# Gated recurrence on one core: bases added by VectorE instead of TensorE, triangular merges moved to GpSimd

## What is computed

```python
def step(carry, inp):
    S, R = carry
    kn = k_t / jnp.maximum(jnp.linalg.norm(k_t, axis=-1, keepdims=True), 1e-12)
    pred = jnp.einsum('bhji,bhj->bhi', S, kn)
    r = jnp.clip(v_t - pred, -CLIP, CLIP)
    S = a_t[..., None] * S
    kp = jnp.einsum('bhd,bhde->bhe', kn, S)
    S = S + b_t[..., None, None] * kn[..., None] * (v_t - kp)[..., None, :]
    o = jnp.einsum('bhji,bhj->bhi', S, q_t)
    R = aR_t[..., None] * R
    kpR = jnp.einsum('bhd,bhde->bhe', kn, R)
    R = R + g_t[..., None, None] * kn[..., None] * (r - kpR)[..., None, :]
    o = o + jnp.einsum('bhji,bhj->bhi', R, q_t)
    return ((S, R), o)
```

## Time and profile before

| | before |
|---|---|
| median of 3 runs | 3105.88 us (3103.14 to 3109.36) |
| the profiled execution, its own time | 3099.7 us |
| its span, first to last instruction | 3097.9 us |
| mean granted clock of TensorE | 0.893 |
| TensorE busy, share of the span | 82% |
| VectorE, ScalarE, GpSimd busy | 68%, 46%, 19% |

### The profile page before, as it was taken

One profiled execution on the slowest core, in us unless ns is written; L12 is line 12 of the kernel. 1 busy time (PEld: TensorE's weight loads), 2 busy tenths in 40 slices (PEclk: granted clock), 3 DMA queues, 4 the chain that ended last, 5 costly groups with the idle time before them and its releaser, 6 DMA issues. The chain is left out here.

```text
span 3097.9 us, 119998 instructions
## 1 busy us (share of the span) xinstructions
PE 2553.5 (82%) x52187; PEld 1910.8 (62%) x52187; DVE 2096.4 (68%) x5265; ACT 1412.9 (46%) x3330; POOL 591.5 (19%) x656
## 2 busy tenths in 40 slices
PE   8887478999976788888888888769998997797745
PEld 6755464556556667676776766547777554575633
DVE  3447236777749888898888988446777666565742
ACT  5443133444453455444544544437777554464310
POOL 0000525556530000000000000001111441261025
PEclk9978778999988899998999999879999998898865
DMA  3200331111110000000000000002222003152013
GB/s 98 61 1 28 121 102 51 45 57 47 38 53 4 4 4 4 4 4 4 4 4 4 4 4 4 3 9 56 62 62 72 3 3 105 48 118 65 5 45 114
DMA packets 79149, 118.11 MB, mean 38 GB/s; under 512 B 11360, under 2 KB 64240, under 8 KB 78096
## 3 DMA queue, kind: packets, MB, share of 16 engines
q1 hardware_dynamic: 66992, 88.80, 9.2%
q0 software_dynamic: 11696, 22.40, 2.9%
HBM read 98.51 MB, written 16.51 MB: 37 GB/s over the span
## 5 line engine op out<-in xcount | busy, mean ns | idle before, releaser
L3114 PE MATMUL psum<-l1d_rw,l1d_cols 64*32 64x32 f32 (+2 forms) x20480 | 241.1, 214 | 91.9 <-issue 75.3
L3114 PEld LDWEIGHTS psum<-l1d_rw,l1d_cols 64*32 64x32 f32 x20480 | 209.3, 107 | 138.3 <-issue 116.0
L2469 POOL TENSOR_SCALAR l1xs_p<-l1xs_p,l1xs_col 128x257 f32<-128x257 f32 x256 | 233.8, 932 | 204.4 <-DVE l1xs_col L2425 204.4
L1740 POOL TENSOR_SCALAR X<-X,l1f_bias 128x512 f32<-128x512 f32 x4 | 6.2, 1567 | 1148.4 <-DMA l1f_bias<-in_l1f_bias 1148.4
L2390 ACT ACTIVATE l1xs_p<-psum,l1xs_col 128x257 f32<-128x257 f32 x256 | 119.4, 472 | 209.4 <-DVE l1xs_col L2420 203.1
L3372 DVE TENSOR_TENSOR l1d_rw<-l1d_rw,l1d_tots 128x1536 f32<-128x1536 f32 x96 | 143.1, 1491 | 76.0 <-PE psum L3114 75.1
L2888 ACT COPY l1d_ya<-psum 128x512 f32<-128x512 f32 x160 | 92.8, 590 | 204.7 <-PE psum L3154 203.8
L2432 DVE STREAM_TRANSPOSE l1xs_pt<-l1xs_p 128x288 f32<-128x288 f32 x256 | 122.4, 478 | 78.7 <-POOL l1xs_p L2469 78.6
L3051 PE MATMUL psum<-l1d_src,l1d_wp 128*128 128x128 f32 x1024 | 139.3, 293 | 1.3 <-ACT l1d_src L2893 1.3
L2342 PE MATMUL psum<-l1xs_keys,l1xs_qx 128*32 128x257 f32 x2048 | 134.0, 395 | 3.5 <-DVE l1xs_qx L2414 1.9
L2354 PE MATMUL psum<-l1xs_pt,l1xs_vals 32*128 32x512 f32 x1152 | 136.6, 604 | 0.0
(11 more groups left out here) (558 smaller groups left out, 6704.4 us busy)
## 6 DMA issues: line engine op xcount, KB each, us to landing
l2f_w<-in_l2f_w SPq DMA_DIRECT2D x16, 768.0 KB, 4.4
l1xs_vals<-in_ctx_strips SPq DMA_DIRECT2D x16, 576.0 KB, 3.8
l0x_ctxT<-in_ctxT SPq DMA_DIRECT2D x16, 516.0 KB, 3.8
l1xs_keys<-in_ctxT SPq DMA_DIRECT2D x16, 516.0 KB, 4.8
l2x_ctxK<-in_ctxT SPq DMA_DIRECT2D x64, 129.0 KB, 2.1
l2x_ctxV<-in_ctxT SPq DMA_DIRECT2D x64, 129.0 KB, 2.1
l1d_wp<-in_l1d_wp SPq DMA_DIRECT2D x1, 2048.0 KB, 8.2
l2f_acc<-l2f_zero SPq DMA_DIRECT2D x8, 256.0 KB, 3.6
```

Of the source, the lines that this page charges most:

```text
L2469: nc.gpsimd.tensor_scalar(p[:, t % 4, :S2], p[:, t % 4, :S2], col[:, 2, t % 4:t % 4 + 1], None, ALU.mult).then_inc(s["norm"], 1)
L3114: mm = nc.tensor.matmul(k.ps[bank0 + pr + e // per * 2][b * T:b * T + T, e % per * w:(e % per + 1) * w], cols[rr, 2 * n, e * 128 + b * T:e ...
```

## The change

The three products by the identity leave TensorE. VectorE adds the base instead: `corner` reads the PSUM bank and the base and writes `ya`, in place of ScalarE's two copies `t` and `t2`, and `clip` adds `v` before it clips, with a wait between the two. The merges leave VectorE for GpSimd, where the sums along the innermost axis become halving additions (34 instructions a tile); the sign that three of the steps carried is put into ScalarE's gather. `turn_back` on VectorE waits for GpSimd (`inverse`). `corner` stands behind `keep_s(i, 1)` and `keep_s(i, 3)`; in lap 16 `result` moves ahead of `corner`, and the clip and the second corner stand behind `turn_back`.

```diff
-             "norm", "turn", "steps", "resid", "colr", "kr")
+             "norm", "turn", "steps", "resid", "colr", "kr", "merged", "last", "inverse")
...
+            tt = nc.gpsimd.tensor_tensor
+
+            def blocks(x, m):
+
+                return (x.rearrange("p (n x) -> p n x", x=2 * m * (T + 1))[:, :, :2 * m * T]
+                        .rearrange("p n (r c) -> p n r c", c=T))
+
+            def merge(i, m):
+
+                nb, lb, xb = T // (2 * m), blocks(lt, m), blocks(xi, m)
+                lo, hi = slice(0, m), slice(m, 2 * m)
+                t5 = tmp[:, :nb * m * m * m].rearrange("p (n r c k) -> p n r c k", n=nb, r=m, c=m)
+                w4 = wmat[:, :nb * m * m].rearrange("p (n r c) -> p n r c", n=nb, r=m)
+                flat = tmp[:, :nb * m * m * m].rearrange("p (x k) -> p x k", k=m)
+                right = lambda x: x.rearrange("p n k c -> p n c k")
+                left = lambda x, r: x[:, :, r:r + 1, :].to_broadcast([128, nb, m, m])
+                step = Steps(pool, s["merged"], i, 10, {2: 0, 4: 4}[m])
+                for r in range(m):
+                    ins = tt(t5[:, :, r], left(lb[:, :, hi, lo], r), right(xb[:, :, lo, lo]), ALU.mult)
+                step(ins)
+                if m == 4:
+                    step(tt(flat[:, :, :2], flat[:, :, :2], flat[:, :, 2:], ALU.add))
+                step(tt(wmat[:, :nb * m * m], flat[:, :, 0], flat[:, :, 1], ALU.add))
+                for r in range(m):
+                    ins = tt(t5[:, :, r], left(xb[:, :, hi, hi], r), right(w4), ALU.mult)
+                step(ins)
+                if m == 4:
+                    step(tt(flat[:, :, :2], flat[:, :, :2], flat[:, :, 2:], ALU.add))
+                step(tt(xb[:, :, hi, lo], t5[:, :, :, :, 0], t5[:, :, :, :, 1], ALU.add))
+
+            def merge_last(i):
+
+                m = 8
+                lb, xb = blocks(lt, m), blocks(xi, m)
+                lo, hi = slice(0, m), slice(m, 2 * m)
+                w4 = [wmat[:, 64 * n:64 * n + 64].rearrange("p (r c) -> p r c", r=m) for n in range(2)]
+                t4 = [tmp[:, 512 * n:512 * n + 512].rearrange("p (r c k) -> p r c k", r=m, c=m) for n in range(2)]
+                flat = [tmp[:, 512 * n:512 * n + 512].rearrange("p (x k) -> p x k", k=m) for n in range(2)]
+                left = lambda x: x.unsqueeze(2).to_broadcast([128, m, m, m])
+                right = lambda x: x.rearrange("p k c -> p c k").unsqueeze(1).to_broadcast([128, m, m, m])
+                for part_ in range(8):
+                    for n in range(2):
+                        if part_ > 0:
+                            pool.wait_ge(s["last"], i * 14 + 2 * part_ + n - 1)
+                        if part_ == 0:
+                            ins = tt(t4[n], left(lb[:, n, hi, lo]), right(xb[:, n, lo, lo]), ALU.mult)
+                        elif part_ == 4:
+                            ins = tt(t4[n], left(xb[:, n, hi, hi]), right(w4[n]), ALU.mult)
+                        elif part_ in (1, 5):
+                            ins = tt(flat[n][:, :, :4], flat[n][:, :, :4], flat[n][:, :, 4:], ALU.add)
+                        elif part_ in (2, 6):
+                            ins = tt(flat[n][:, :, :2], flat[n][:, :, :2], flat[n][:, :, 2:4], ALU.add)
+                        elif part_ == 3:
+                            ins = tt(wmat[:, 64 * n:64 * n + 64], flat[n][:, :, 0], flat[n][:, :, 1], ALU.add)
+                        else:
+                            ins = tt(xb[:, n, hi, lo], t4[n][:, :, :, 0], t4[n][:, :, :, 1], ALU.add)
+                        ins.then_inc(s["inverse" if part_ == 7 else "last"], 1)
+
+            for i in range(NT):
+                pool.wait_ge(s["turn"], 2 * i + 2)
+                merge(i, 2)
+                merge(i, 4)
+                merge_last(i)
...
-                copy(at[:, :H, :], ms[:, i % 2, :, 0, :])
-                copy(at[:, H:, :], mr[:, i % 2, :, 1, :]).then_inc(s["kc"], 1)
+                nc.scalar.mul(at[:, :H, :], ms[:, i % 2, :, 0, :], -1.0)
+                nc.scalar.mul(at[:, H:, :], mr[:, i % 2, :, 1, :], -1.0).then_inc(s["kc"], 1)
...
                     take(i - 2, "y_mm", ya, "A", "y")
-                    take(i - 2, "z_mm", ya, "B", "t")
...
-                if old:
-                    take(i - 2, "z2_mm", ya, "B", "t2")
...
-                apply(i, "B", wide(3), ya, "z_mm", v)
+                apply(i, "B", wide(3), ya, "z_mm")
...
-                apply(i, "B", wide(0), u, "p_mm", v)
+                apply(i, "B", wide(0), u, "p_mm")
...
-                apply(i, "B", wide(4), ya, "z2_mm", rd)
+                apply(i, "B", wide(4), ya, "z2_mm")
...
-                t(vc.tensor_scalar(first(xi), first(lt), -1.0, None, ALU.mult))
+                t(vc.tensor_copy(first(xi), first(lt)))
 
             def turn_back(i):
+                dve.wait_ge(s["inverse"], 2 * i + 2)
                 vc.transpose(kc[:], xi[:, :T * T]).then_inc(s["back"], 1)
+
+            def corner(i, mm, base, done):
+                for j in range(2):
+                    dve.wait_ge(s[mm], i * 2 + j + 1)
+                    at = slice(j * 512, j * 512 + 512)
+                    tt(ya[:, at], k.ps[bank("B") + j][:], base[:, at], ALU.add).then_inc(s[done], 1)
 
             def clip(i):
                 for j in range(2):
                     dve.wait_ge(s["p_mm"], i * 2 + j + 1)
                     if i > 0:
                         dve.wait_ge(s["out_mm"], i)
-                    vc.tensor_scalar(rd[:, j * 512:(j + 1) * 512], k.ps[6 + j][:], 1.0, -1.0, ALU.min, ALU.max
-                                     ).then_inc(s["r"], 1)
+                    at = slice(j * 512, j * 512 + 512)
+                    step(tt(rd[:, at], k.ps[6 + j][:], v[:, at], ALU.add))
+                    vc.tensor_scalar(rd[:, at], rd[:, at], 1.0, -1.0, ALU.min, ALU.max).then_inc(s["r"], 1)
 
             def result(i):
                 dve.wait_ge(s["out_mm"], i + 1)
@@ -3541,15 +3571,13 @@
                     advance_r(i, 0)
                     advance_s(i, 1)
                     keep_s(i, 1)
-                if mid:
-                    merge(2)
+                if i == NT:
+                    result(i - 3)
+                if old:
+                    corner(i - 2, "z_mm", v, "t")
                 if now:
                     advance_r(i, 1)
                     keep_r(i, 1)
-                if mid:
-                    merge(4)
-                if i == NT:
-                    result(i - 3)
                 if now:
                     advance_s(i, 2)
                 if old and i != NT:
@@ -3558,21 +3586,21 @@
                     keep_s(i, 2)
                     advance_r(i, 2)
                     keep_r(i, 2)
-                if mid:
-                    merge_last(0)
                 if now:
                     advance_s(i, 3)
                     keep_s(i, 3)
+                if old and i != NT:
+                    corner(i - 2, "z2_mm", rd, "t2")
+                if now:
                     advance_r(i, 3)
                     keep_r(i, 3)
-                if mid:
-                    merge_last(1)
                 if new:
                     norms(i + 1)
                 if mid:
                     turn_back(i - 1)
                 if i == NT:
                     clip(i - 2)
+                    corner(i - 2, "z2_mm", rd, "t2")
                 if now:
                     keep_s(i, 4)
                 if new:
```

More of the change, by code:

```diff
@@ L2843, in l1_attn @@
         kc, lt, xi = sb("kc", [128, T * T]), sb("lt", [128, T * (T + 1)]), sb("xi", [128, T * (T + 1)])
-        tmp, wmat = sb("tmp", [128, 1024]), sb("wmat", [128, 64])
+        tmp, wmat = sb("tmp", [128, 1024]), sb("wmat", [128, 128])
         block = ph.enter_context(nc.Block())
@@ L3457, in keep_r @@
                 ins.then_inc(s["mR"], 1)
-            def blocks(x, m):
-                return (x.rearrange("p (n x) -> p n x", x=2 * m * (T + 1))[:, :, :2 * m * T]
-                        .rearrange("p n (r c) -> p n r c", c=T))
             def turn(i):
@@ L3469, in turn @@
                 t(vc.transpose(lt[:, :T * T], kc[:]))
-                t(vc.tensor_scalar(first(xi), first(lt), -1.0, None, ALU.mult))
-            def merge(m):
-                nb, lb, xb = T // (2 * m), blocks(lt, m), blocks(xi, m)
-                lo, hi = slice(0, m), slice(m, 2 * m)
-                t5 = tmp[:, :nb * m * m * m].rearrange("p (n r c k) -> p n r c k", n=nb, r=m, c=m)
-                w4 = wmat[:, :nb * m * m].rearrange("p (n r c) -> p n r c", n=nb, r=m)
-                flat = tmp[:, :nb * m * m * m].rearrange("p (x k) -> p x k", k=m)
-                right = lambda x: x.rearrange("p n k c -> p n c k")
-                left = lambda x, r: x[:, :, r:r + 1, :].to_broadcast([128, nb, m, m])
-                for r in range(m):
-                    ins = tt(t5[:, :, r], left(lb[:, :, hi, lo], r), right(xb[:, :, lo, lo]), ALU.mult)
-                step(ins)
```

(19 more changed lines are left out.)

## The result

| | before | after |
|---|---|---|
| median | 3107.62 us (4 runs) | 3064.81 us (3054.27 to 3071.25, 4 runs) |
| ratio, 95% interval | | 0.9858 (0.983 to 0.9885) |
| profiled execution | 3099.7 us | 3071.25 us, clock 0.887 |
| turn(1) to turn(15), 14 laps | 931.0 us | 900.8 us |
| turn(15) to the last result | 73.1 us | 67.1 us |

A forecast was written before the change was run, and what follows sets the result against it. Neither TensorE nor VectorE plainly bound; the prediction read TensorE as running dry between instruction packets, shown as "issue" time. Terms -3 - 27 + 18 - 6 = -18 gave a median of 3088 us, range 3050 to 3124.

The forecast's parts named there:

- The bases, -27: Fourteen steady laps: dropping TensorE's identity products gains 1.1 us in each of eight short laps, 3 in six long ones.
- the 1.4 to 1.6 of the text: Sign that the forecast is right: u starts 1.4 to 1.6 us after keep_s(i, 1) in nearly all laps.
- long lap: Six of fourteen steady laps, where TensorE is late and step_u starts 4.4 us after VectorE began its first merge.
- Both engines at once, +18: Steady laps: VectorE multiplies delayed by GpSimd working beside them cost 1.3 us a lap, 18 us in 14 laps.
- the ceiling: Each VectorE multiply with two SBUF inputs waits for GpSimd's instruction in flight: 4.5 us a short lap, 2.5 a long one.
- Its own test: VectorE multiplies (1.76 and 1.23 us) unchanged and without gaps refute exclusion by GpSimd; if they stretch, the prediction is wrong.
- rival 1: VectorE and GpSimd exclude each other, costing 51 us instead of 18: 3121 us, slower; chance 0.22.
- Since TensorE waits for VectorE hardly anywhere, this pays only in lap 1: Merges removed from VectorE gain only in lap 1, half of its 5.66 us wait for the norms: -3 us.
- rival 5: With less TensorE work the clock falls, giving back 1 to 2 us a lap: 3105 us, no change; chance 0.07.
- Laps 16 and 17, -6: The last two laps: lap 16 gives +0.4 and -1.8, lap 17 -4.8, together -6 us.
- Rival 2: Instruction packets bind nothing, contention costs nothing, up to 91 us from 48 identity pairs: 3010 to 3050 us; chance 0.12.
- Rival 4: GpSimd needs over 39 us a tile, stalling VectorE at turn_back: at 45 us, 90 us on top, 3180; chance 0.05.

The follow-up runs named there:

- e11: The changed kernel without its merges, but with 14 multiplies of 512 columns a tile on GpSimd that nobody waits for; ratio 1.0099 to the kernel before.
- e1: The kernel before with the bases alone changed: VectorE adds them by corner and clip, merges stay on VectorE; ratio 0.9907 to the kernel before.
- e4: The changed kernel with GpSimd's merges cut to two small multiplies a tile, inverse left out; ratio 0.9827 to the kernel before.
- e14: The kernel of e4 measured a second time; ratio 0.9792 to the kernel before.
- e5: The kernel before with the merges left out on every engine, identity products kept; ratio 0.9901 to the kernel before.
- e15: The kernel before without merge_last(1), the 3.6 us merge right ahead of the norms; ratio 0.9935 to the kernel before.
- e3: The kernel before with the identity products left out and nothing in their place; ratio 0.9864 to the kernel before.
- e6: The kernel before with both the merges and the identity products left out, nothing in their place; ratio 0.9794 to the kernel before.

## Why the prediction was right and wrong

1. **The bases, -27: right in size.** Alone they gave 24.2 us in 14 laps. `step_u` started 1.1 to 1.2 us after `keep_s(i, 1)` in twelve of 14 laps and 1.4 in two, near the 1.4 to 1.6 of the text. What the text did not have is the clock: its long lap's identity pair of 3.63 us ran at a granted clock of 0.54, the one of 1.98 at 1.00.
2. **Both engines at once, +18: right in size as far as is known (15 in the traces, 0 to 24 by the medians), for a partly wrong reason.** Each VectorE multiply does wait for the GpSimd instruction in flight, as the ceiling had it; the time stays below the ceiling of 51 because most of these are short, and because VectorE waits afterwards (41.4 us for fills at L3432 in 910). Its own test, multiplies unchanged or stretched, would have said rival 1, at 3121. GpSimd was stretched too, to 25 us a tile where the text had 18, and this cost nothing in the steady laps. e11 shows that rival as real when GpSimd's instructions are long.
3. **"Since TensorE waits for VectorE hardly anywhere, this pays only in lap 1": wrong, and the whole miss.** The merges' absence from VectorE is worth 24.7 us from e1 to e4 and e14 in the 14 laps, and 30 alone (e5). Lap 1 gave 0.9 instead of 3 (turn(1) at 1040.8 and 1041.7). The prediction had the wait of 5.66 us at L3104 in lap 1 and took the steady laps to be free of it. Thirteen waits of 1.4 us, 18.1 in all, stood a few rows below the one that it showed. It also compared the engines only at `step_u`, in the middle of the lap, where TensorE is late in long laps; at the end of every lap it is VectorE that is late. And it gave a relief no effect on the clock but a bad one (rival 5). Of the 24.6 us of e15, 13.4 are TensorE's idle time and 11.2 its busy time at a higher granted clock.
4. **Laps 16 and 17, -6: right.** 73.1 to 65.9 us (mean of three), -7.2; GpSimd's chain from the end of turn(15) to `turn_back` took 17.1 us there, where VectorE is mostly idle, against the 18 assumed.

The sum, mended: -0.9 - 24.2 - 24.7 + 14.8 - 7.2 = -42.2. Its three middle terms are steps of one chain, before to e1 to e4 and e14 to the changed kernel, so they add up to the difference of its ends whatever each of them is worth; and the reliefs overlap (e5 has 30 for the one that is 24.7 here). It is made of single executions with a spread of about 10 us in 14 laps, and before was profiled in one only, 8 us under its median in this comparison, so that the match with -42.8 is closer than the terms allow. Rival 2's time (3010 to 3050) is refuted: with the identity left out e3 has 42 us and not 91. TensorE was busy for 80 us less there and idle for 39 more, and its idle time put down to "issue" rose from 82 to 127 us, as the prediction's reading has it; whether packets make it is open. Rival 4 did not come: `turn_back` never waited for GpSimd in the steady laps. Rival 5 came in part: the clock of the stretch fell from 0.94 to 0.92, as with the bases alone (0.91 in the laps of e1), but the relief of VectorE raised it again (0.94 in e14), and the gain was still there. What sets the floor of about 882 us, which e4, e6 and e14 share, is not settled; TensorE is busy for 702 to 710 us of it and idle for 174 to 178.

## What to carry to other kernels

Before calling an engine's work free, list every wait that ends on it, not only the longest one of the other engine: a short wait that recurs in each lap is worth its sum, and here more: 13 us less of waiting brought 25, because TensorE's granted clock was higher without it. Compare busy times of the same instructions too, not only waits. When work must go between two steps of a serial chain, put it where its engine would wait for something else; exchanging it past that point cost 33 us here for a piece of 3.6. Work moved to GpSimd beside VectorE multiplies should come in short instructions: about the same GpSimd time a tile (25 us) cost 84 us in 14 laps in pieces of 512 columns, and some 15 in the merges' mostly shorter ones.
